# Attention on one core: maxima begin at step 8 instead of 10 with their transfers ahead of the inverses', the last block counted on TensorE without a sum, and probability buffers given out by a table

## The reference

```python
q = _heads(x @ Wq, B, L, nh, hd)
kv_s = x @ Wkv_short
decay_bias = -jnp.abs(pos[None, :] - pos[:, None]) * (1.0 - decay_factor)
out_short = _attention(q, k_s, v_s, decay_bias)   # softmax(q k^T / sqrt(hd) + bias) v
kv_l = x @ Wkv_long
out_long = _attention(q, k_l, v_l, None)
alpha = jax.nn.sigmoid(mix_weight)
out = alpha * out_short + (1.0 - alpha) * out_long
return out.transpose(0, 2, 1, 3).reshape(B, L, H) @ Wo
```

## Time and profile before

| | |
|---|---|
| median of 3 runs | 4771.02 us (4766.81 to 4774.06) |
| profiled execution | 4764.1 us, span 4762.1 us |
| attention stage | about 488 to 3650 us of the span |
| TensorE / VectorE / GpSimd / ScalarE busy, whole span | 94% / 80% / 65% / 63% |

### The profile page before, as it was taken

One profiled execution on the slowest core, in us unless ns is written; L12 is line 12 of the kernel. 1 busy time (PEld: TensorE's weight loads), 2 busy tenths in 40 slices (PEclk: granted clock), 3 DMA queues, 4 the chain that ended last, 5 costly groups with the idle time before them and its releaser, 6 DMA issues. The chain is left out here.

```text
span 4762.1 us, 157195 instructions
## 1 busy us (share of the span) xinstructions
PE 4467.5 (94%) x61452; PEld 2434.6 (51%) x61452; DVE 3788.4 (80%) x4400; ACT 2982.2 (63%) x5297; POOL 3088.7 (65%) x1236
## 2 busy tenths in 40 slices
PE   8999799999999999999999999999995899999998
PEld 3444244444444555444444444444442677777776
DVE  7657788888888888888888888888781688888887
ACT  3222377777777777777777777777774455555553
POOL 0000389898989898988989888889885333333332
PEclk9999699999999999999999999999997899999999
DMA  5444376767666667667767666676754000000000
GB/s 168 138 127 123 86 150 139 156 143 153 144 146 142 151 146 156 137 145 146 151 144 151 143 144 144 144 153 144 151 107 117 21 28 21 28 28 21 28 23 12
DMA packets 242106, 547.41 MB, mean 115 GB/s; under 512 B 71471, under 2 KB 145327, under 8 KB 200561
## 3 DMA queue, kind: packets, MB, share of 16 engines
q0 software_dynamic: 45792, 333.47, 35.4%
q1 hardware_dynamic: 195563, 203.94, 15.0%
q10 hardware_dynamic: 38, 0.08, 0.0%
HBM read 140.34 MB, written 62.16 MB: 43 GB/s over the span
## 5 line engine op out<-in xcount | busy, mean ns | idle before, releaser
L983 DVE TENSOR_REDUCE rowmax_parts<-scores_qk 128x1 f32<-128x1024 f32 x2048 | 2414.8, 1218 | 514.4 <-PE scores_qk L1068 509.7
L961 ACT ACTIVATE probs_T<-scores_kq 128x512 f32<-128x512 f32 x3840 | 2069.3, 602 | 535.0 <-PE scores_kq L1068 379.0
L868 POOL TENSOR_TENSOR probs_added<-probs_added,probs_T 128x2048 f32<-128x2048 f32 x446 | 2093.9, 4695 | 48.0 <-POOL probs_added L868 38.1
L1068 PE MATMUL scores_kq<-q_operand,k_operand 103*32 103x512 f16 (+3 forms) x13312 | 1239.5, 372 | 126.5 <-DMA q_operand_above<-negmax_T 68.8
L1068 PE MATMUL scores_qk<-k_operand,q_operand 96*32 96x512 f16 (+4 forms) x13312 | 1050.7, 373 | 27.9 <-DMA v_operand<-v_dram 14.2
L1150 PE MATMUL outputs_T<-probs_T,v_operand 128*32 128x512 f32 x7680 | 1029.1, 598 | 6.4 <-issue 5.6
L1068 PEld LDWEIGHTS scores_kq<-q_operand,k_operand 103*32 103x32 f16 x13312 | 396.5, 96 | 692.5 <-ACT probs_T L961 275.8
L1068 PEld LDWEIGHTS scores_qk<-k_operand,q_operand 102*32 102x32 f16 (+1 forms) x13312 | 385.9, 98 | 512.6 <-issue 229.8
L1758 PE MATMUL f_gate_up<-w_gate_up,xq_T 128*128 128x256 f16 (+1 forms) x4608 | 494.2, 266 | 7.6 <-DVE hidden L1649 6.5
L868 POOL TENSOR_TENSOR probs_added<-probs_T 128x2048 f32<-128x2048 f32 x64 | 292.0, 4563 | 292.4 <-DVE probs_T L1012 239.3
L1758 PEld LDWEIGHTS f_gate_up<-w_gate_up,xq_T 128*128 128x128 f16 x4608 | 421.0, 98 | 77.0 <-issue 24.3
(11 more groups left out here) (173 smaller groups left out, 4570.0 us busy)
## 6 DMA issues: line engine op xcount, KB each, us to landing
probs_poured<-probs_T POOLq DMA_DIRECT2D x318, 1024.0 KB, 8.7
qk_parts_dram<-qk_parts SPq DMA_DIRECT2D x96, 256.0 KB, 2.8
q_operand<-qk_parts_dram SPq DMA_DIRECT2D x192, 128.0 KB, 3.4
k_operand<-qk_parts_dram SPq DMA_DIRECT2D x192, 128.0 KB, 7.4
v_dram<-v_heads SPq DMA_DIRECT2D x16, 1024.0 KB, 6.4
v_operand<-v_dram SPq DMA_DIRECT2D x64, 256.0 KB, 6.7
sums_inverse<-sums_inverse_dram SPq DMA_DIRECT2D x64, 256.0 KB
q_operand_above<-qk_parts_dram SPq DMA_DIRECT2D x96, 128.0 KB, 4.1
```

The lines of the kernel that those rows point to most:

```text
L868: nc.gpsimd.tensor_tensor(total, first, block_of(w, b), ALU.add).then_inc(added.sem, 1)
L961: nc.scalar.activation(block_of(w, kb)[:, qt * BANK:(qt + 1) * BANK], pb[:, ring_of(c) % BANKS, :], ACT.Exp).then_inc(expd.sem, 1)
L983: nc.vector.reduce_max(rowmax[:, w % 2, g // 2, g % 2:g % 2 + 1], half, AX.X).then_inc(maxed.sem, 1)
L1068: mm = nc.tensor.matmul(out[j:j + HD, :], lhsT[:, j:j + HD], rhs, start=start, stop=stop, skip_group_check=True)
```

## The change

`ASTEPS` and `TURN_MAX` go from 10 to 8, so the maxima of the unit after next begin two steps earlier and those of the next unit are turned two steps earlier; `EARLY` goes from 24 to 32 chunks. In SyncE's list `place_max` comes before `store_inverse`. Block 14 is added by DMA instead of by GpSimd, and block 15, which was added by DMA, is added by nobody: `count_added` multiplies it with ones into the same bank as probs_added (`RAW`). The weighing is behind block 13. Buffers: block 14 has one to itself, the other fourteen share seven, in order, so blocks 8 to 13 take the buffers of 1 to 6 and block 15 that of 7. `block_free` follows the table and for block 15's buffer waits for that count.

```diff
-ASTEPS = 10
+ASTEPS = 8
-TURN_MAX = 10
+TURN_MAX = 8
-BY_DMA = (1, 6, 9, 12, 15)
+BY_DMA = (1, 6, 9, 12, 14)
-BY_POOL = (3, 4, 5, 7, 8, 10, 11, 13, 14)
+BY_POOL = (3, 4, 5, 7, 8, 10, 11, 13)
+RAW = KB - 1
-POOL_ORDER = (1, 4, 5, 6, 7, 8, 9, 10, 11, 12, 13, 14, 15)
-WEIGH_BEHIND = 14
+POOL_ORDER = (1, 4, 5, 6, 7, 8, 9, 10, 11, 12, 13, 14)
+WEIGH_BEHIND = 13
+ALONE = 14
+SLOT = {b: k % (PBUF - 1) for k, b in enumerate(b for b in range(1, KB) if b != ALONE)} | {ALONE: PBUF - 1}
...
-            return poured_sum[:, w % 2, :] if kb == 0 else probs[:, kb % PBUF, :]
+            return poured_sum[:, w % 2, :] if kb == 0 else probs[:, SLOT[kb], :]
...
                         for j in range(2):
                             pack_sums(*back, j)
-                        store_inverse(*back)
                     if after(w, n, last):
                         place_max(*after(w, n, last))
                     if back:
+                        store_inverse(*back)
                         spread_inverse(*back)
...
-                u, b = (w, kb - PBUF) if kb > PBUF else (w - 1, kb + PBUF) if kb < PBUF else (w - 1, kb)
+                same = [b for b in range(1, KB) if SLOT[b] == SLOT[kb]]
+                u, b = (w, same[0]) if kb > same[0] else (w - 1, same[-1])
                 act.wait_ge(summed.sem, summed.at(n, u * KB + b + 1))
                 if b == JOINED[0]:
                     act.wait_ge(joined.sem, joined.at(n, u + 1))
+                elif b == RAW:
+                    act.wait_ge(counted[0].sem, counted[0].at(n, u + 1))
...
-                count(pb[:, COUNT_SLOTS[0] % BANKS, :], added_sum[:, w % 2, :], True, True).then_inc(counted[0].sem, 1)
+                bank = pb[:, COUNT_SLOTS[0] % BANKS, :]
+                count(bank, added_sum[:, w % 2, :], True, False)
+                count(bank, block_of(w, RAW), False, True).then_inc(counted[0].sem, 1)
```

## The result

The changed kernel takes 4779.78 us (median of 20 runs, 4765.34 to 4797.64), the kernel before 4769.24 (20 runs, of which the ratio leaves out one of 22184 us): a ratio of 1.0027 [1.0017, 1.0038]. It is 10 to 13 us slower, where 64 us less were predicted and 0.82 of the chance stood on faster than before. The profiled execution took 4765.34 us, the fastest of the 20, so its waits are, if anything, on the short side.

A forecast was written before the change was run, and what follows sets the result against it. TensorE was taken to set the pace at 48.05 us a unit; less 1.6, 0.6 and 0.3, plus 0.86 and 0.55, gains 1.10. Over 62 units, less 3.8 at the ends: 64 us, 4707 us; range 4650 to 4766.

The forecast's parts named there:

- Maxima earlier: Turning maxima at step 8, transfers first, ends TensorE's wait at step 14; 1.6 us a unit saved, half clock included.
- the early transfers are slowed: Rival: maxima transfers at steps 8 to 10 slowed beside a DMA sum, half the wait stays; 4731 us, chance 0.16.
- the wait isn't the transfers': Rival: TensorE's step 14 wait has another cause; near 0 a unit, 4775 us, part of the no-change case, chance 0.08.
- The inverse's later store: On SyncE the inverse's store goes some 7.4 us later, behind eight transfers; cost taken as 0.
- The count: Block 15's direct count at step 4 adds 0.86 us a unit on TensorE, less 0.3 in a shadow behind DVE's join.
- ScalarE's waits before blocks 4 and 7: ScalarE's waits for landings of DMA sums before these blocks both go; 0.6 us a unit saved on TensorE.
- The new wait d: Block 8 waits for block 1's DMA sum to land; d = 47.5 - P, P the unit's time; 0.55 us a unit.
- The boundary wait: TensorE's wait at step 14 of odd units for the maxima's transfers; 57.9 us in 28 cases, to be removed.
- Half clock: TensorE at half clock after long waits, 40.7 us in all; 0.36 us a unit returned with the wait at step 14.
- The prologue: 32 instead of 24 chunks of unit 1's maxima before the loop, paced by DVE; 4.7 us more.
- GpSimd's queue becomes the clock: Rival: longer landings of DMA sums delay block 1 and lengthen units; 60 us slower, 4831 us, chance 0.09.
- Lands in time: Rival: block 12's DMA sum lands 2 us earlier, so d is 0; 105 us gained, 4666 us, chance 0.22.

The follow-up runs named there:

- g2: g1 with the store of the inverse ahead of the maxima's transfers in SyncE's list again; 4773.19 us, 1.0015 of the kernel before.
- g1: Kernel before with early maxima, their transfers first, block 1's DMA sum behind block 13's sum, block 15 alone in its buffer, no direct count; 4641.69 us.
- e8: e5 without the direct count of block 15, whose values are missing from the sums; 4650.57 us.
- e5: Changed kernel with the DMA sum of the next unit's block 1 issued behind the weighing, ahead of block 14's; 4678.84 us.
- e3: Changed kernel with the maxima at step 10 again and the inverse's store ahead of their transfers; 4784.9 us.
- f1: Changed kernel with 0.87 us of repeated score work in steps 12 and 13 of odd units only; 4774.57 us.
- f3: Changed kernel with 2.6 us of repeated score work in steps 12 and 13 of odd units only; 4800.54 us.
- e1: Changed kernel with the buffer of its own given to block 1 instead of block 14; 4701.5 us.
- e4: Changed kernel without the DMA sum of block 14, whose values are missing from the sums; 4671.3 us.
- f4: Changed kernel with 2.6 us of repeated score work in steps 12 and 13 of even units only; 4862.65 us.
- e2: Kernel before with only the maxima at step 8 and their transfers ahead of the inverse's store; 4726.91 us.
- e6: e5 with the loads of q, k and v of passes after the first cut to 128 columns; 4679.03 us.
- e7: e5 with the buffer of its own given to block 1 instead of block 14, as in e1; 4778.0 us.

## Why the prediction was wrong, step by step

**What bounds it.** Right: TensorE sets the pace; a clean step is 2.60 us still (the median of each of the odd units' steps 8 to 13).

**Maxima earlier.** Right: in unit 21 the turn (L1003), the issues and the next need are at 1591.65, 1591.96 to 1598.62, and about 1604 (two steps before 1609.79). The timelines of VectorE and SyncE, then the landings of the transfers of negmax_T:

```profile
1591.65 0.20 DVE L1003 STREAM_TRANSPOSE negmax_T<-negmax 128x32 f16<-128x32 f16 x1
...
1591.96 3.22 SPq L770 DMA_DIRECT2D q_operand<-negmax_T  x4
1595.22 3.40 SPq L770 DMA_DIRECT2D q_operand_above<-negmax_T  x4
...
DMA to landing us min/median/max: 1.6/2.3/7.1
```

No wait for them is left, and g2 against g1 shows the new order to be worth 131 us with its half clock (85.3 us of it in g2, over units 4 to 60); the 1.6 a unit of the prediction is 99. The rivals that the early transfers are slowed, or that the wait isn't the transfers', both fell. The inverse's later store costs nothing, as taken.

**The count.** 1.71 us long as said, +0.86. The shadow is 0.42 where 0.3 was taken (bounds 0 and 0.5): e8 measures 28 us where 0.56 a unit in 64 would be 36.

**ScalarE's waits before blocks 4 and 7.** Right: steps 5 and 6 both last 2.71 us in even and 2.66 in odd units (medians), where unit 21 had 3.15 in step 5 before.

**The new wait d. This step failed**: "P = 46.4 + 47.5 - P, so P = 46.95 and d = 0.55". Its numbers were good. From the start of unit 19 block 12's DMA sum is issued at +44.2 (44.8 worked out), lands at +55.6 (55.1), and block 1's lands at +69.6 (68.5). What was wrong is to solve for one common unit. A wait can't be negative, and the landing ties each unit to the one before: d(n), the wait in unit n, is max(0, 47.5 - P(n-1)). Started anywhere but at 0.55 this doesn't settle: a short unit gives the next one a long wait, a long one gives it none. If odd and even units were alike without d, the mean would still be 0.55 (1.1 and 0 in turn). They are not: without d the odd ones take 45.64, the even ones 48.20 (e5). So all the waiting is the even units', and the prediction's own formula gives them 47.5 - 45.64 = 1.9, which is 0.95 a unit. Measured: over the even units block 1's DMA sum lands on average 23.5 us into the unit, and 23.5 - 21.0 = 2.5; step 7 lasts 5.72 us on average there against 3.60 clean, 2.1 more, and 3.85 in odd units. That is 1.1 a unit, twice the predicted 0.55. The tie to the unit before shows in single units: step 7 takes 6.6 us in the mean of the 17 even units whose odd unit before was under 46 us, and 4.3 in the 11 others. The mean of the earlier trace rows runs over both kinds of unit, and step 14 in the earlier trace rows already showed them unlike.

What follows is that the pair has a fixed length, from the odd unit's start to that landing in the even one (69.6 in units 19 and 20, 68.2 to 70.6 in all 28) and then the rest of the even one. The boundary wait stood in the odd unit, ahead of that landing, so its removal gives next to nothing (e3 to changed: the pair 97.1 to 96.7), and a padding there costs little (f1; f3 until the wait is used up). Shown by e1, e5, e4 (three cures, 78 to 108 us) and f3 against f4.

**Half clock.** 0.36 us a unit were taken as given back with the boundary wait. In the changed kernel eleven stretches show a clock of 0.50 or 0.51, 44.2 us in all where it was 40.7. One behind a wait at L1163 (unit 22), one at a wait for "issue" (unit 32), and the sum (length; busy PE, PEld, DVE, ACT, POOL; granted clock, DMA share, GB/s):

```profile
1634.70:1638.10 3.40, 3.40 (x35) 1.33 (x30) 1.00 (x1) 2.10 (x5) 3.40 (x2) 0.50 0.77 157
...
2098.90:2105.70 6.80, 5.05 (x48) 1.81 (x52) 1.23 (x1) 2.28 (x4) 1.74 (x2) 0.50 0.44 102
...
sum 44.20, PE 41.67 PEld 18.50 DVE 14.88 ACT 22.52 POOL 36.61; mean PE 3.79 PEld 1.68 DVE 1.35 ACT 2.05 POOL 3.33
```

Six of the eleven follow waits before the count (1.9 to 3.7 us), four follow waits for "issue" (1.8 to 4.9 us), one a wait for VectorE. The clock follows the wait wherever it goes. e5, without d, has 10.2 us of it.

**"Issue".** It was 18.0 and two small rows of the kernel before:

```profile
PE outputs_T L1150 <- issue: 3.4, 1, 3.4
PE scores_qk L1068 <- issue: 2.7, 4, 1.5
```

24.1 us in all; now 48.2. The prediction had no term for its growth.

**The sum of it.** In units 4 to 60, -61.6 was predicted and +17.1 came, 78.7 apart: some 28 of it is d (28 x 2.1 instead of 56 x 0.55), some 20 the half clock (which overlaps with d where it lies in step 7), 24 "issue". e5 divides it without an overlap: against the changed kernel it gives back 2.9 us a pair, 80 us in these units, where the prediction had 31 for d, so the landing with all that follows from it makes 49 of the 78.7; the other 29 are in e5 too, 15 of them more waits for "issue" (39.2 us against 24.1). Behind unit 60 the execution is 18.3 us shorter (1312.9 against 1331.2), where 3 was predicted; some 7 of it are waits of the last unit of the kernel before, of which the changed kernel has 3.8 us in 14 cases, none over 0.3:

```profile
PE scores_kq L1068 <- ACT probs_T L961: 11.0, 11, 6.0
```

The prologue is 5 us longer (unit 0 starts at 554.3, before at 549.3), as said.

**The rivals.** "GpSimd's queue becomes the clock" (0.09) is the nearest to what happened, and its price was right in kind: what block 1's landing costs decides the sign. It needed no longer landings, though; the worked-out one was enough. "Lands in time" fell: 12's landed in 11.4 us, block 1's in 12.7. The Trainium skill, page "DMA: Bandwidth & Descriptors", section "Anatomy of one DMA — SWDGE (gpsimd) path", has about 2.0 us and the bytes at 436 GB/s, by which an estimate for 1 MB is 4.4 us. The trace does not agree for these accumulating transfers, with its 11.4 and 12.7 us.

## What to carry to other kernels

Where a wait depends on the unit before, write it as max(0, ...) for each kind of unit in turn, with that kind's own floor, and not as one mean solved for itself; a late landing dated from one unit pins the pair, and then what is saved ahead of it is given back at it. Before you take a wait away, look for the next one in line on the same path and cure it first (e2 alone -40; with block 1's sum moved forward and block 15 alone in its buffer as well, g1, -128). A step moved earlier on one engine is worth nothing if its transfers stand behind a waiting instruction on the queue that issues them (g2).

## What the runs showed of the hardware

TensorE's waits for "issue" sit at fixed places of the code. The loop has rounds of 28 units, and the same wait comes back a round later; units 28 and 56 of the changed kernel, 33 us into the unit:

```profile
1930.26 0.62 PE L1156 MATMUL outputs_T<-probs_T,v_operand 128*32 128x512 f32 x2 [1.82 <-issue]
...
3290.91 0.62 PE L1156 MATMUL outputs_T<-probs_T,v_operand 128*32 128x512 f32 x2 [1.83 <-issue]
```

Each edit moves them: 24 us before, 28 to 48 in the others, over units 4 to 60 of each. They can be long (4.87 us in unit 32) and then take half clock with them. Smaller loads did not change them (e6).

The traces tell more of them. The profile's list of DMA queues has one called instruction (q8), whose packets have 16 KB each. In the changed kernel all 39 "issue" waits of units 4 to 60 end 1.25 to 1.67 us behind the end of such a packet, and in the sixteen kernels together all 588 end 1.15 to 1.90 us behind one; of random moments only some 11% lie 1.1 to 1.9 us behind one. The longest of them, then the queues (packets, MB, share of the 16 engines) in the first part of that wait, 2095.7 to 2098, where the instruction queue has no packet, and in the next, 2098 to 2099.3, where it has one:

```profile
2100.65 0.40 PE L1074 MATMUL scores_kq<-kink_kq,ident_f 128*32 128x128 f16 x8 [4.87 <-issue]
...
q0 software_dynamic: 55, 0.45, 97.0%
...
q8 instruction: 1, 0.02, 5.2%
```

So these are waits for TensorE's own instructions, as far as times alone can show it. The Trainium skill, page "Runtime: NRT & Kernel Launch", section "Instruction fetch mechanics", has instructions fetched in blocks of 16 KB by the sequencer's own DMA queue, at a cost that is mostly hidden in code without branches. The trace agrees in the main: of 377 such packets in units 4 to 60, 39 are waited for, 1.2 us each on average. What makes those late stays open. In the 4 us before a packet that is waited for, GpSimd's queue of DMA sums (q0) fills 85% of the 16 engines' time, before the others 61%; but no run takes that traffic away at these places.

A transfer of the maxima lands the sooner the earlier in the unit it is issued: 2.3 us (median of all) in the changed kernel, 2.4 to 2.8 in e1, e2, e5, e7 and g1, but 3.5 to 3.6 before, in e3 and in g2, where SyncE gets to them at step 10. g2 turns them at step 8 like g1, so it is the place of the issue that counts. Which traffic they meet there was not tried. The DMA sums went the other way, a median of 9.1 us from 8.7.
